# Static zero rows ahead of each expert's queue, in place of zero rows written behind the counted ends, in a routed three-layer block on one core

## The reference

```python
x = layernorm(x + dilated_attention(x))              # 16 heads, segments of 64, every second token
x = layernorm(x + cross_attention(x, ctx_512, ...))  # 16 heads, causal, 128 latent rows
x = layernorm(x + moe_ffn(x, gate_w, w_gate, w_up, w_down))

# moe_ffn: T = 2048, E = 32 experts, K = 8, C = 2 * (T * K // E) = 1024
probs = softmax(x @ gate_w);  w, sel = top_k(probs, K);  w = w / sum(w)
# every (token, choice) goes to its expert's queue, in token order, at most C per expert
y = (silu(xg @ w_gate) * (xg @ w_up)) @ w_down       # per expert, 256 -> 96 -> 256
out[token] += w * y
```

## Time and profile before

| | us |
|---|---|
| median of 3 runs | 622.9 (622.82 to 624.33) |
| the profiled execution, its own time | 623.45 |
| its span, first to last instruction | 621.8 |
| PE busy | 512.0 (82%) |
| POOL busy | 399.8 (64%) |
| DVE busy | 367.2 (59%) |
| ACT busy | 335.4 (54%) |

### The profile page before, as it was taken

The page is one execution under the profiler, slowest core; times in us unless marked ns, Lnnn a source line. Parts: engine busy times, 40 slices in busy tenths (PEclk is TensorE's granted clock), DMA queues, the critical chain, the costliest instruction groups (busy, mean ns, idle before and its releaser), DMA issues.

```text
span 621.8 us, 17381 instructions
## 1 busy us (share of the span) xinstructions
PE 512.0 (82%) x5065; PEld 393.7 (63%) x5066; DVE 367.2 (59%) x1527; ACT 335.4 (54%) x1204; POOL 399.8 (64%) x604
## 2 busy tenths in 40 slices
PE   2888998888888888885119999999999999994994
PEld 2555555555555555542008888888888888883773
DVE  1468787777777787763304555555555555552664
ACT  2266666666666666663005666666666666661112
POOL 6553666666666666556715777777777768774653
PEclk9599999999999999996558999999999999996998
DMA  9999999932222222222785656656655556666994
GB/s 196 281 242 311 343 341 338 337 135 84 74 74 84 74 79 80 77 85 90 260 272 164 183 177 180 185 171 189 188 180 176 179 171 186 186 180 249 427 418 153
DMA packets 82301, 121.30 MB, mean 195 GB/s; under 512 B 13011, under 2 KB 71901, under 8 KB 80224
## 3 DMA queue, kind: packets, MB, share of 16 engines
q1 hardware_dynamic: 64896, 79.51, 42.0%
q0 software_dynamic: 14016, 38.44, 17.4%
q10 hardware_dynamic: 3360, 2.98, 1.5%
HBM read 56.07 MB, written 69.01 MB: 201 GB/s over the span
## 4 chain that ended last, share of the span: by engine, by line
PE 42%; POOL 16%; issue 14%; DVE 12%; DMA 6%; ACT 5%; ACTq 3%; POOLq 1%; SPq 1%; DVEq 0%
PE bank L796 16%; PE bank L812 11%; POOL queues L533 10%; PE bank L788 7%; DMA wall<-results 4%; DVE kP L1048 3%; ACT pr L873 3%; PE bank L806 3%; ACTq L297 2%; POOL rz L498 1%; POOL rz L492 1%; POOL pair_z L569 1%; DVE nmax L1025 1%; PE bank L614 1%; PE bank L604 1%
## 5 line engine op out<-in xcount | busy, mean ns | idle before, releaser
L559 POOL DMA_INDIRECT results<-ys,wcol x152 | 150.2, 988 | 26.2 <-POOL pscrap L548 24.1
L533 POOL DMA_INDIRECT queues<-x,xidx x128 | 128.5, 1004 | 37.2 <-issue 36.3
L796 PE MATMUL bank<-wall,xtT 128*128 x616 | 127.0, 329 | 0.1
L873 ACT ACTIVATE pr<-bank,nmax 128x128 f32<-128x128 f32 x256 | 90.9, 370 | 29.1 <-DVE nmax L1025 29.1
L796 PEld LDWEIGHTS bank<-wall,xtT 128*128 128x128 f32 x616 | 98.5, 194 | 0.5 <-issue 0.5
L966 ACT ACTIVATE ys<-bank,wcol 128x256 f32<-128x256 f32 x152 | 72.1, 474 | 44.5 <-PE bank L812 44.5
L1219 DVE SCALAR_TENSOR_TENSOR tg<-th,bank 128x96 f32<-128x96 f32 x154 | 39.1, 254 | 90.8 <-ACT th L960 90.6
L788 PE MATMUL bank<-ident,xt 128*128 128x128 f32 x310 | 63.4, 286 | 34.2 <-DMA xt<-queues 22.9
L812 PE MATMUL bank<-wall,hT 96*128 x304 | 90.8, 380 | 0.0
L788 PEld LDWEIGHTS bank<-ident,xt 128*128 128x128 f32 x310 | 59.2, 198 | 48.7 <-DMA xt<-queues 23.9
L604 PE MATMUL bank<-kP,qS 128*128 128x512 f32 x128 | 67.1, 606 | 0.0
(11 more groups left out here) (178 smaller groups left out, 879.6 us busy)
## 6 DMA issues: line engine op xcount, KB each, us to landing
xt<-queues SPq DMA_DIRECT2D x162, 160.0 KB, 2.2
results<-zeros SPq DMA_DIRECT2D x16, 1024.0 KB
wall<-results SPq DMA_DIRECT2D x16, 1024.0 KB, 13.9
queues<-zeros SPq DMA_DIRECT2D x32, 160.0 KB, 2.8
wall<-in_L_ffn_w_gate SPq DMA_DIRECT2D x4, 768.0 KB, 11.5
wall<-in_L_ffn_w_up SPq DMA_DIRECT2D x4, 768.0 KB, 13.6
wall<-in_L_ffn_w_down SPq DMA_DIRECT2D x4, 768.0 KB, 13.0
results<-ys,wcol POOLq DMA_INDIRECT x152, 2.6
```

Of the source, the lines that this page charges most:

```text
L533: pool.indirect_dma_start(xg, bass.IndirectOffsetOnAxis(ap=xidx[:, par, k:k + 1], axis=0), x2[:, par, :], None, bounds_check=last_row, oob ...
L559: pool.indirect_dma_start(yr, bass.IndirectOffsetOnAxis(ap=wcol[:, u, 1:2], axis=0), ys[:, u, :], None, bounds_check=last_y, oob_is_err=Fa ...
L796: ins = pe.matmul(bank[2 + u % 2][:, 0:2 * INTER].rearrange("p (g i) -> p g i", g=2), xtT[:, u % 2, kk, :], wall[:, bass.ds(e, GU)].rearrange(
L873: ins = act.activation(pr[:, g % 2, q, :], pS[g % 2][:, q * P:(q + 1) * P], ACT.Exp, bias=nmax[:, 4 * g + q:4 * g + q + 1], accum_out=den[ ...
```

## The change

Each expert's 1152 rows are divided anew: the 128 zero rows lie in front, at fixed places, and tokens start behind them. The zeros are written by four fixed transfers of SP's early zeros (eight experts each). A block now ends where the queue ends: an expert's first block starts so many rows early that the last one is full, and reaches into the zeros in front. The idle region moves by 128 rows. `pad_queues`, `tab_p`, `eoff` and the semaphore `pad_late` go.

The tables change with it. A block's first row is now counted in rows, and must take off the rows that its expert's queue lacks to full blocks: two columns `lackb` (DVE), a matrix `begun` beside `past` (DVE), and two more products into the same sum (PE).

```diff
-IDLE rows at NE * STRIDE + k * P              (XG_ROWS = NE * STRIDE + IDLE * P)
+IDLE rows at NE * STRIDE + (k + 1) * P        (XG_ROWS = NE * STRIDE + (1 + IDLE) * P)
-PADS = (14, 28)
+PADS = 4
 # SP, early zeros, between the idle region and the results
+            heads = xg[0:NE * STRIDE, :].rearrange("(e s) w -> s e w", s=STRIDE)
+            for k in range(PADS):
+                n = NE // PADS
+                sp.dma_start(heads[0:P, n * k:n * (k + 1), :],
+                             zeros[:, :].unsqueeze(1).to_broadcast([P, n, XW])).then_inc(pad_zero, 16)
 # SP, after the early zeros
-            sp.wait_ge(dveH.sem, dveH.at(0, "tp"))
-            pad_queues(sp, ET.SP, 0, PADS[0], pad_zero)
             sp.wait_ge(dveH.sem, dveH.at(0, "tx"))
...
-            sp.wait_ge(pad_zero, 16 * PADS[1])
-            sp.wait_ge(pad_late, 16 * (NE - PADS[1]))
+            sp.wait_ge(pad_zero, 16 * PADS)
 # POOL constants
-                put(pool.iota, eoff_i[:, :], [[STRIDE, NE]], base=0, channel_multiplier=0)
+                put(pool.iota, eoff_i[:, :], [[STRIDE, NE]], base=P, channel_multiplier=0)
-                put(pool.tensor_copy, eoff[:, :], eoff_i[:, :])
 # POOL after the last tokens
-            pool.wait_ge(dveH.sem, dveH.at(0, "tp"))
-            pad_queues(pool, ET.Pool, PADS[1], NE, pad_late)
 # ACT after the attention stage
-            act.wait_ge(dveH.sem, dveH.at(0, "tp"))
-            pad_queues(act, ET.Activation, PADS[0], PADS[1], pad_zero)
 # PE tables
-                pe.matmul(pW[0:1, 96:96 + NE], onesb[:, 0:1], seen[:, :], start=True, stop=True)
-                pe.wait_ge(dveH.sem, dveH.at(0, "skipb"))
+                pe.wait_ge(dveH.sem, dveH.at(0, "nblkb"))
...
-                pe.matmul(pW[0:1, 326:326 + TAB], skipb[:, :], past[:, :], start=True, stop=True
+                pe.matmul(pW[0:1, 326:326 + TAB], skipb[:, :], past[:, :], start=True, stop=False)
+                pe.matmul(pW[0:1, 326:326 + TAB], lackb[:, 0:1], past[:, :], start=False, stop=False)
+                pe.matmul(pW[0:1, 326:326 + TAB], lackb[:, 1:2], begun[:, :], start=False, stop=True
 # DVE tables: rows in place of blocks; tab_p goes, two lackb and begun come
-                dve.tensor_tensor(tab_p[0:1, :], pW[0:1, 96:96 + NE], eoff[0:1, :], ALU.add).then_inc(s, 1)
+                dve.scalar_tensor_tensor(lackb[:, 0:1], nblk[:, :], float(P), took[:, :], ALU.mult, ALU.subtract
+                dve.scalar_tensor_tensor(lackb[:, 1:2], nblk[:, :], -float(P), took[:, :], ALU.mult, ALU.add
+                dve.tensor_scalar(begun[:, :], blk[:, :], nblk[:, 0:1], cum[:, 0:1], ALU.add, ALU.is_ge)
```

More of the change, by code:

```diff
@@ L33 @@
 IDLE = 2 * UN + 2
-XG_ROWS = NE * STRIDE + IDLE * P
+XG_ROWS = NE * STRIDE + (1 + IDLE) * P
 Y_ROWS = NB * P * TOPK
@@ L46 @@
 B_CONST = FIRST_CONST + 23
-N_CONST = 54
+N_CONST = 53
 assert MAXB % UN == 0
@@ L118, in build @@
         eoff_i = sb("eoff_i", [P, NE], I32)
-        eoff = sb("eoff", [P, NE])
         ufar = sb("ufar", [P, NE])
@@ L187, in build @@
         past = sb("past", [NE, TAB], BF16)
+        begun = sb("begun", [NE, TAB], BF16)
+        lackb = sb("lackb", [NE, 2], BF16)
         tjunk = sb("tjunk", [1, MAXB // UN])
@@ L192, in build @@
         tab_x = sb("tab_x", [1, TAB + 2 * LEAD], I32)
-        tab_p = sb("tab_p", [1, NE], I32)
         tab_n = sb("tab_n", [1, 1], I32)
@@ L237, in build @@
         peH = Steps(sem("peH"), "count place table")
-        dveH = Steps(sem("dveH"), "took tp nblk nblkb skipb cum past n n2 fe fx tg tw tx")
+        dveH = Steps(sem("dveH"), "took nblk nblkb skipb lack over cum past begun n n2 fe fx tg tw tx")
         peF = {n: sem(f"peF_{n}") for n in ("xT", "gu", "hT", "y")}
@@ L253, in build @@
         pad_zero = sem("pad_zero")
-        pad_late = sem("pad_late")
         yr_zero = sem("yr_zero")
@@ L291, in neighbours @@
                 skip_runtime_bounds_check_because="the tables hold rows and columns of these arrays only")[1]
[L293 to L297, removed]
         def store(eng, b):
@@ L329, in _ @@
             for k in range(IDLE):
-                r = NE * STRIDE + k * P
+                r = NE * STRIDE + (k + 1) * P
                 sp.dma_start(xg[r:r + P, :], zeros[:, :]).then_inc(idle_zero, 16)
+            heads = xg[0:NE * STRIDE, :].rearrange("(e s) w -> s e w", s=STRIDE)
[3 more added lines that the diff above has]
+                             zeros[:, :].unsqueeze(1).to_broadcast([P, n, XW])).then_inc(pad_zero, 16)
             for b in range(NB):
@@ L1179, in tables @@
                 dve.tensor_copy(nblkb[:, :], nblk[:, :]).then_inc(s, 1)
-                dve.tensor_scalar(skipb[:, :], nblk[:, :], -1.0, float(STRIDE // P), ALU.mult, ALU.add).then_inc(s, 1)
+                dve.tensor_scalar(skipb[:, :], nblk[:, :], -float(P), float(STRIDE), ALU.mult, ALU.add).then_inc(s, 1)
+                dve.scalar_tensor_tensor(lackb[:, 0:1], nblk[:, :], float(P), took[:, :], ALU.mult, ALU.subtract
+                                         ).then_inc(s, 1)
+                dve.scalar_tensor_tensor(lackb[:, 1:2], nblk[:, :], -float(P), took[:, :], ALU.mult, ALU.add
+                                         ).then_inc(s, 1)
                 dve.wait_ge(peH.sem, peH.at(0, "place"))
@@ L1184, in tables @@
                 dve.tensor_scalar(past[:, :], blk[:, :], cum[:, 0:1], None, ALU.is_ge).then_inc(s, 1)
+                dve.tensor_scalar(begun[:, :], blk[:, :], nblk[:, 0:1], cum[:, 0:1], ALU.add, ALU.is_ge).then_inc(s, 1)
                 dve.tensor_scalar(tjunk[:, :], blk[0:1, 0:MAXB:UN], pW[0:1, 130:131], 0.0, ALU.is_lt, ALU.add,
@@ L1191, in tables @@
                                   ).then_inc(s, 1)
-                dve.tensor_tensor(tab_f[0:1, 1, :], pW[0:1, 326:326 + TAB], blk[0:1, :], ALU.add).then_inc(s, 1)
+                dve.scalar_tensor_tensor(tab_f[0:1, 1, :], blk[0:1, :], float(P), pW[0:1, 326:326 + TAB],
+                                         ALU.mult, ALU.add).then_inc(s, 1)
                 dve.wait_ge(s, H("fe"))
@@ L1197, in tables @@
                 dve.wait_ge(s, H("fx"))
-                dve.tensor_scalar(tab_x[0:1, LEAD:LEAD + TAB], tab_f[0:1, 1, :], float(P), None, ALU.mult
+                dve.tensor_scalar(tab_x[0:1, LEAD:LEAD + TAB], tab_f[0:1, 1, :], float(P), None, ALU.add
                                   ).then_inc(s, 1)
```

## The result

The changed kernel took 612.57 us (median of 4 runs, 611.88 to 615.37), the kernel before 622.86 us in the same comparison (622.35 to 624.33): a ratio of 0.9836, 95% interval 0.9804 to 0.9867. The forecast was 612.7 us. The profiled execution of the changed kernel is the longest of its runs, 615.37 us with a span of 613.4; what follows compares it with the one before, 623.45 us.

A forecast was written before the change was run, and what follows sets the result against it. The seam's wait for zero rows was taken to hold the first load and the end behind it; 623.45 - 10.45 = 613.0 us, or 612.45 against the median, forecast 612.7, own range 610.5 to 616 (stated range 610.4 to 616.5).

The forecast's parts named there:

- What bounds the seam: Between attention and expert stage, SP's wait for zeros landing at 321.52 holds the first load, at 321.81, with DMA engines full.
- The tokens' landing: At the seam, POOL's last token transfer lands 2.09 us after 308.98, as with nearly idle engines; first load 10.45 us earlier.
- SP's table loads: At the seam, three loads take 4.52 us and end at 307.5, some 3.6 us ahead of the tokens' landing.
- The tables' shift: On DVE and PE ahead of the loads, added and removed table pieces finish the tables 0.45 us later, hidden.
- The early zeros: In the attention stage, 5.24 MB more in SP's queue, 15.4 us at full engines, costs 0, at most 0.25 us.
- rival at the slot of `x2`: In the attention stage, full engines delay token transfers until DVE waits at L1082: slower, 628 us at an 18 us landing; 3 in 100.
- The expert stage: Same number of blocks, products and transfers, only blocks' first rows differ: change in length taken as 0.
- bound of the clock: TensorE's low clock at the expert stage's start, 6 us long, could shrink by up to 3; taken as 0.
- POOL's gap: Between token transfers at the attention stage's end, POOL's unexplained 2.48 us standstill may go or recur: up to 2.2 us either way.
- landing of 7.6 us: Rival at the seam: the tokens' landing stays as long as with full engines, total 618.5 us; 6 in 100.
- table loads of 5.06 each: Rival at the seam: SP's three loads become the wait, first load at 318.44, total 620.1 us; 5 in 100.
- change without effect: Rival at the seam: another wait holds the first load at 321 or later, about 623 us; 4 in 100.

The follow-up runs named there:

- late_full: Changed kernel with 32 zero transfers of 160 KB put back at the seam, at fixed rows, waited for before the first block load: 622.79 us, ratio 0.9989.
- late_8: Changed kernel with the same 5.24 MB of zeros put back at the seam in 8 transfers of 640 KB, waited for: 622.34 us, ratio 0.9983.
- late_free: Changed kernel with 32 zero transfers at the seam to rows nobody reads, waited for only after the expert stage: 624.21 us, ratio 0.9999.
- again: The changed kernel run once more, unedited: 614.59 us, ratio 0.9849 to the kernel before, over 6 runs.
- tables_16: Changed kernel with 16 DVE additions of 128x512, SBUF to SBUF, put ahead of `tab_x`: 622.24 us, ratio 0.9966.
- tables_ps16: Changed kernel with 16 one-input DVE maxima over a PSUM bank added to delay the tables: 615.66 us, ratio 0.9867.
- early_x4: Changed kernel with twelve more zero transfers of 1280 KB, to rows nobody reads, behind the four early ones: 613.7 us, ratio 0.9831.
- warm_26: Changed kernel with 26 PE products of 128x512 into an unused bank between the last table product and the first block: 613.83 us, ratio 0.9831.
- warm_42: Changed kernel with 42 PE products of 128x512 behind the table products, to last until the first block: 614.75 us, ratio 0.9848.

## Why the prediction was right

The mechanism was the one predicted; single terms were mis-sized, and two of them cancelled.

- **What bounds the seam.** Right, and late_full and late_8 show it: with the bytes back the gain is gone, in 32 transfers or 8. The prediction put it on SP's wait for the landing. late_free shows that to be too narrow: without that wait SP's own issues and table loads hold the load nearly as late.
- **The tokens' landing.** Right in kind, mis-sized: 2.50 us where 2.09 was taken from the quiet row. again and tables_16 show 2.50 and 2.49. The Trainium skill's estimate of 2.38, which the prediction set aside ("DMA: Bandwidth & Descriptors", section "Anatomy of one DMA — SWDGE (gpsimd) path"), was nearer. The 0.41 was made up by the transfer being issued 0.58 earlier (308.40 against 308.98), which no term held, and by 0.22 in place of 0.29 behind the landing, so the load at 311.12 is 0.24 ahead of the predicted 311.36. The 0.58 came with the attention stage's earlier end and, as far as the runs show, is luck: the seam itself gained 10.03 us where 10.45 was forecast.
- **SP's table loads.** 2.1 us for the three (302.2 to 304.3) where 4.52 was taken over from full engines. The cover was therefore 6.6 us and not 3.6; tables_ps16 used it up and the load moved by what was left over.
- **The tables' shift.** From the end of `xidx` to the end of `tab_x` 3.59 us against 3.32: 0.27 where 0.45 was taken. Hidden, as predicted.
- **The early zeros.** 0, as predicted; early_x4 with four times the bytes still shows it. The rival at the slot of `x2` falls: the steps did not change.
- **The expert stage.** Taken as 0, it lost 2.25 us in the profiled execution, which had 10.9 us of low clock in place of 6.0. The prediction had that as a bound of the clock (up to 3) and set 0 as its value. Another 0.32 went outside the span, where 1.97 us lie now and 1.65 before; all runs of the changed kernel have 1.96 to 2.1 there, those of the kernel before 1.61 to 1.74, and the cause is not shown. So the profiled execution gained 8.08 us. Between the medians 10.3 us were gained, near the first load's 10.69; in the comparison of again it was 8.9. That 612.57 lies so near the forecast of 612.7 is more than the terms deserve: the shorter attention stage and the longer expert stage were not in the sum.
- **POOL's gap.** It neither went nor came: 2.14 us against 2.48.
- **The other rivals.** The landing of 7.6 us, table loads of 5.06 each and a change without effect would have put the first load at about 316.9, 318.4 and 321 or later; it went out at 311.12.

## What to carry to other kernels

Writes that depend on no data belong where the DMA queues have room, not into the seam between two stages: at a seam they fill the engines, and with them slow everything that the next stage waits for, so that removing only the wait for them gained nothing in the time here. After such a cut the next wait is read from the same chain, here the last token landing behind POOL's eight transfers of 1.28 us each, and then the engine that issues the first load, which was through with its table loads 6.6 us sooner. When a cover is measured by an added delay, the delay must not touch the other side: look first whether the other engine's rows kept their length.

## What the hardware showed that was not expected

- A run of DVE additions from SBUF held one of POOL's indirect transfers for its whole length, 4.49 and 10.53 us against 0.97. Maxima from PSUM, for as long, did not (0.97 to 0.98).
- SP's table loads took 0.53 to 0.67 us with quiet DMA engines (changed kernel), 1.08 to 2.06 behind zeros at full engines (late_free), and one on ACT took 5.06 before.
- With zero transfers of 64 rows (80 KB) the engines moved 245 GB/s at a share of 0.99, with those of 128 rows (160 KB) 345 at 1.03 (token transfers included).
- The clock fell from 1.00 to 0.50 in the first blocks although PE had just worked for 8.64 and 11.46 us at a stretch (then 3.73 us idle in warm_26, waits of up to 0.86 us in warm_42), and PE's low level lasted from 5 to 12 us after its first product among kernels that issue the same blocks.
